# Last mixture of a vision tower: who adds the normalised input, and who adds up the two output sums

## The reference

```python
def _moe(tokens, router_w, w1, b1, w2, b2):
    logits = tokens @ router_w.T
    probs = softmax(logits)
    rw, re = top_k(probs, 2)
    rw = rw / max(rw.sum(-1), 1e-12)
    combine = zeros((N, E)).at[arange(N)[:, None], re].set(rw)
    out = tokens
    for e in range(E):
        hid = gelu(tokens @ w1[e] + b1[e])
        y = hid @ w2[e] + b2[e]
        out = out + combine[:, e:e + 1] * y
    return out
h = h + _moe(_layernorm(h), ...)
```

## Time and profile before

| | |
|---|---|
| median of 3 runs | 734.87 us (733.46 to 735.16) |
| profiled execution | 733.23 us, its span 731.4 us |
| busy over the span | PE 606.9 us (83%), DVE 503.9 (69%), ACT 319.3 (44%), POOL 141.2 (19%) |
| mean granted TensorE clock | 0.928 of full speed |

### The profile page before, as it was taken

How to read it: one execution, slowest core, us unless ns; L and a number is a source line. 1 busy time by engine, 2 the same in 40 slices (tenths; PEclk the granted TensorE clock), 3 DMA queues, 4 the chain that set the end, 5 groups by cost and what they waited for, 6 DMA issues and landing times. The chain is left out here.

```text
span 731.4 us, 17563 instructions
## 1 busy us (share of the span) xinstructions
PE 606.9 (83%) x6943; PEld 377.2 (52%) x6943; DVE 503.9 (69%) x1451; ACT 319.3 (44%) x739; POOL 141.2 (19%) x151
## 2 busy tenths in 40 slices
PE   2999999699975977888887979999955968889884
PEld 2875655489863333444432347787743434444441
DVE  3767789357764547777667327878857688988863
ACT  0100011043322665666665628877941453444441
POOL 1000000465443103221003032431314012220000
PEclk9999999989995799999998899999965799999998
DMA  9998870000000000000000000000000000000001
GB/s 310 411 366 278 293 286 3 1 2 2 2 2 0 1 1 2 2 1 1 3 1 1 1 1 2 2 1 3 1 2 0 5 16 14 17 19 21 20 23 26
DMA packets 28898, 39.19 MB, mean 54 GB/s; under 512 B 19985, under 2 KB 20369, under 8 KB 28817
## 3 DMA queue, kind: packets, MB, share of 16 engines
q1 hardware_dynamic: 19232, 35.46, 13.5%
q10 hardware_dynamic: 9584, 2.61, 1.8%
HBM read 35.37 MB, written 2.69 MB: 52 GB/s over the span
## 5 line engine op out<-in xcount | busy, mean ns | idle before, releaser
L423 POOL TENSOR_TENSOR centred<-h,mean 82x512 f32<-82x512 f32 x64 | 67.4, 1052 | 497.6 <-DVE rstd L412 299.6
L1226 ACT ACTIVATE m_h<-bank,m_b 128x656 f32<-128x656 f32 x112 | 90.4, 807 | 130.2 <-PE bank L1333 130.0
L1556 DVE TENSOR_TENSOR m_hm<-bank,m_h 128x656 f32<-128x656 f32 x112 | 93.7, 836 | 70.5 <-PE bank L1343 70.5
L283 PE MATMUL bank<-cols,tok_weight 64*64 64x328 f32 (+1 forms) x1800 | 114.4, 411 | 16.8 <-DVE cols L321 15.3
L283 PEld LDWEIGHTS bank<-cols,tok_weight 64*64 64x64 f32 x1800 | 76.0, 136 | 52.1 <-issue 17.1
L1333 PE MATMUL bank<-m_xt,m_w 64*64 64x328 f32 x896 | 94.4, 494 | 9.6 <-ACT m_h L1226 8.7
L320 DVE COPY cols<-image 128x1992 f32<-128x1992 f32 x32 | 62.2, 1952 | 16.8 <-DMA image<-in_x_dram 14.7
L1333 PEld LDWEIGHTS bank<-m_xt,m_w 64*64 64x64 f32 x896 | 24.8, 139 | 57.5 <-issue 28.2
L1366 PE MATMUL bank<-m_hm,m_wo 64*64 64x328 f32 x512 | 49.8, 459 | 2.7 <-DVE m_osb L1563 2.3
L813 ACT ACTIVATE sa_prob<-sa_masked,sa_low 82x82 f32<-82x82 f32 x128 | 44.6, 350 | 8.5 <-DVE sa_low L948 8.5
L1343 PE MATMUL bank<-ct,m_sel 64*64 64x328 bf16 x448 | 37.7, 318 | 12.6 <-DVE m_hm L1556 12.2
(11 more groups left out here) (172 smaller groups left out, 1060.9 us busy)
## 6 DMA issues: line engine op xcount, KB each, us to landing
image<-in_x_dram SPq DMA_DIRECT2D x32, 1000.0 KB, 11.1
out_dram<-m_fin SPq DMA_DIRECT2D x16, 164.0 KB
tok_weight<-in_L_tok_weight_dram ACTq DMA_DIRECT2D x2, 400.0 KB, 8.2
m_w<-in_L_ffn_w_dram ACTq DMA_DIRECT2D x2, 128.0 KB
m_sel_raw<-c_sel_dram ACTq DMA_DIRECT2D x1, 256.0 KB
m_w<-in_L_ffn_expert_w_dram ACTq DMA_DIRECT2D x2, 96.0 KB
m_wo<-in_L_ffn_expert_w_dram ACTq DMA_DIRECT2D x4, 48.0 KB
m_sel_raw<-c_sel_dram ACTq DMA_DIRECT2D x1, 192.0 KB
```

Source lines behind the costliest of these rows:

```text
L283: return pe.matmul(sum_bank[u % 2][s][t * D:(t + 1) * D, L * j0:L * j1], weight[s * R:(s + 1) * R, c, :], cols[u % 2][s * R:(s + 1) * R, c ...
L423: pool.tensor_tensor(self.centred[:], slots(self.h, g), mean.broadcast_to([L, G, D]), ALU.subtract).then_inc(self.shifted, 1)
L1226: act.activation(h1[n % RING][:], h1_bank, ACT.Gelu if last else ACT.Relu, bias=W.b1[:, k:k + 1]).then_inc(h1_ready, 1)
L1556: dve.tensor_tensor(hm[k][:], cb_bank, src[n % RING][:], ALU.mult).then_inc(hm_ready, 1)
```

## The change

Pool adds the normalised group to `h` in place (`widen`), right before it normalises the group three further on; the last three follow at the end. VectorE then no longer adds `xt` in `output`: ScalarE copies the even sums from PSUM into a new tile `even` (`output_even`), and VectorE makes `osb` from the odd sums and `even` in one step. `residual` waits for `widened` as well. `copy_x` waits for `h1_done` in both mixtures.

```diff
--- before.py
+++ after.py
@@ -1117,6 +1117,7 @@
         h2 = None if last else [sb(f"h2_{n}", [128, 2, HALF]) for n in range(RING)]
         hm = [sb(f"hm{k}", [128, 2, HALF]) for k in range(NP)]
         osb = sb("osb", [128, HALF])
+        even = sb("even", [128, HALF]) if last else None
         unused = sb("unused", [L, 1])
 
         lg = [sb(f"lg{p}", [L, 2 * G, E]) for p in (0, 1)]
@@ -1154,6 +1155,7 @@
         o_pairs = sem("o_pairs")
         o_done = sem("o_done")
         o_even = sem("o_even")
+        widened = sem("widened")
         o_ready = sem("o_ready")
         o_turned = sem("o_turned")
         added = sem("added")
@@ -1176,11 +1178,21 @@
 
             @block.gpsimd
             def _(pool):
+                def widen(f):
+
+                    pool.wait_ge(normed, f + 1)
+                    pool.tensor_tensor(slots(h, f), slots(h, f), mine.rows(f), ALU.add).then_inc(widened, 1)
+
                 def step(f):
+                    if last:
+                        widen(f - AHEAD)
                     wait(pool, x_turned, f - 2)
                     mine.normalise(pool, f)
 
                 in_groups(step, AHEAD)
+                if last:
+                    for f in range(NG - AHEAD, NG):
+                        widen(f)
                 if following is not None:
                     pool.wait_ge(normed, NG)
                     for f in range(AHEAD):
@@ -1191,10 +1203,7 @@
 
                 def copy_x(f):
                     act.wait_ge(x_turned, f + 1)
-                    if last:
-                        wait(act, o_ready, f - FRONT - 1)
-                    else:
-                        wait(act, h1_done, (f - FRONT - 1) * NP)
+                    wait(act, h1_done, (f - FRONT - 1) * NP)
                     act.activation(xt[f % len(xt)][:], front[:, 0:HALF], ACT.Copy).then_inc(x_ready, 1)
 
                 def router_hidden(f):
@@ -1232,6 +1241,11 @@
                     for s in (0, 1):
                         ins = act.activation(h2[n % RING][:, s, :], h2_bank[:, s, :], ACT.Relu, bias=W.b2[:, s, k:k + 1])
                     ins.then_inc(h2_ready, 1)
+
+                def output_even(g):
+                    act.wait_ge(o_done, g + 1)
+                    wait(act, o_ready, g)
+                    act.activation(even[:], o_banks[0], ACT.Copy).then_inc(o_even, 1)
 
                 def output(g):
                     act.wait_ge(o_done, g + 1)
@@ -1261,6 +1275,8 @@
                             hidden1(g, k + 1)
                         elif exists(g + 1):
                             hidden1(g + 1, 0)
+                        if k == 0 and last and exists(g - 1):
+                            output_even(g - 1)
                         if not last:
                             hidden2(g, k)
                             if k == 0:
@@ -1281,7 +1297,9 @@
                     LayerNorm.after_act(act, g, mine, following)
 
                 in_groups(step)
-                if not last:
+                if last:
+                    output_even(NG - 1)
+                else:
                     output(NG - 1)
 
             @block.tensor
@@ -1558,12 +1576,13 @@
                 def output(g):
                     dve.wait_ge(o_done, g + 1)
                     wait(dve, o_turned, g)
-                    dve.tensor_tensor(osb[:], o_banks[0], xt[g % len(xt)][:], ALU.add).then_inc(o_even, 1)
                     dve.wait_ge(o_even, g + 1)
-                    dve.tensor_tensor(osb[:], o_banks[1], osb[:], ALU.add).then_inc(o_ready, 1)
+                    dve.tensor_tensor(osb[:], o_banks[1], even[:], ALU.add).then_inc(o_ready, 1)
 
                 def residual(g):
                     dve.wait_ge(o_turned, g + 1)
+                    if last:
+                        dve.wait_ge(widened, g + 1)
                     if last and g >= 2:
                         dve.wait_ge(sent[g % 2], g // 2 * 16)
                     dst = fin[g % 2][:] if last else slots(h, g)
```

## The result

The changed kernel takes 757.05 us (754.36 to 760.33, six runs), the kernel before, run beside it, 734.66 us (733.46 to 735.16, six runs): a ratio of 1.031 [1.028, 1.033], 22.4 us slower. The profiled execution took 755.29 us, its span is 753.5 us where it was 731.4. In the later runs 14 of 60 executions of the kernel before took 742 to 752 us, at a lower mean clock; medians are of all executions, and ratios with their intervals of those at most 1.5% above the fastest of their kernel.

The account below looks back on a forecast made before the run. Bound in the last stage by TensorE's spread, VectorE's routing steps stretched by Pool, and the product. Start 3.2, cast bursts 1.64, ranking bursts 1.53, less 0.8 for the sums: +5.6 us, 740.5 us; range 736.5 to 745.5.

Parts of the forecast that it names:

- Direction and place: Last stage: slower by 0.75%, because Pool's adds hold up VectorE's routing steps and TensorE waits for the product.
- One sign: Expected trace sign in the last stage: the period of steps 4 to 8 longer by half a microsecond to 0.8.
- The rival that ends on the other side, the output path wins: Adds shift off the routing steps, only the output sums' gain is left: up to -2.6 us, 732.3 us; chance 0.06.
- the 0.8 us that I summed: Output sums: TensorE's late waits for osb shrink by 0.52, 0.26, 0.03 and about 0.03 us, together -0.8 us.
- Pool's add at 1.04 us: Each of Pool's 16 new 82x512 adds takes 1.04 us, bounds 1.04 and 1.15.
- cast block: Cast bursts: Pool's add stretches VectorE's L1548 from 0.29 to 1.11 us, 0.82 us each, twice.
- ranking block: Ranking bursts: Pool's add delays the end of VectorE's L1522 from 655.18 to 655.69, 0.51 us, three times.
- The start at +3.2 us: Last stage's start: four of six adds each block one more VectorE routing step, 4 x 0.79 us; bounds 1.6 to all four.
- the bursts at 1.64 + 1.53: Adds as third Pool instruction block VectorE's routing: two cast bursts cost 1.64 us, three ranking bursts 1.53; 3.2 in all.
- my 5.6: Whole change: the start's 3.2, cast bursts' 1.64 and ranking bursts' 1.53 less 0.8 for the sums, +5.6 us.
- The clock: TensorE's clock in the last stage: no loss in the forecast sum, though waits for the product grow to 2.0 to 2.1 us.
- two or three more such falls: Rival: TensorE's clock falls two or three more times in the last stage, +3.6 to +5.4 us, 744 to 746; chance 0.15.

Follow-up runs that it names:

- filled pair: The changed kernel and the kernel before, each with six useless TensorE matmuls ahead of the wait for hm in steps 3 to 8: 743.05 and 736.51 us.
- The adds in mid-step: The changed kernel with Pool's adds from group 8 on waiting until a step's output is ready, normalisations unmoved: 749.73 us, ratio 1.017 to the kernel before.
- half-width adds: The changed kernel with each Pool add over half of its group only (82x256): 741.56 us, ratio 1.009 to the kernel before.
- eight tiles with the old normalisations: The changed kernel with eight xn buffers and only the adds moved to mid-step, Pool's normalisations in their old place: 734.65 us, ratio 1.001 to the kernel before.
- filled kernel: The changed kernel with six useless TensorE matmuls ahead of the wait for hm in steps 3 to 8: 743.05 us, ratio 1.012 to the kernel before.

## Why the prediction was wrong in size

*Direction and place.* Right. The adds alone cost as much as the whole change (757.47), everything else gives back 0.8 to 1.5 us (733.65), the blocked steps are L1566 and L1540, and the reduction beside them runs free. One sign failed clearly: the period of steps 4 to 8 was to grow by half a microsecond to 0.8, and went from 10.0 to 10.2 us to 13.3 to 13.5.

*The rival that ends on the other side, the output path wins.* Its mechanism is there, worth the 0.8 us that I summed: osb waits went from 2.3 us to 1.5. Its premise, that the adds shift away from the routing steps, did not come true.

*Pool's add at 1.04 us.* Mis-sized: 1.31 us in the median, 1.26 to 1.39. The adds have two full inputs, the two rows that I took it from read a full and a broadcast one. What follows from the Trainium skill's cycles an element (GPSIMD Engine Reference, 3.1 Elementwise), an estimate of 1.11 us, is short as well; the measurement decides. It made the cast block 0.95 us for 0.82, and the ranking block 0.63 for 0.51.

*The start at +3.2 us and the bursts at 1.64 + 1.53.* The start measured +3.6. The waits for hm grew by 0.13 us in step 3, 0.55 in step 4, 0.95 in each cast step and 0.61 in each ranking step, 3.8 us for my 3.2. With -0.8 this makes 6.6 us for my 5.6, and the filled pair measures 6.5.

*The clock.* This is the step that failed. The sum put the clock at nothing. I wrote that "elsewhere after waits of 1.25 to 1.5 us it stays at 2.4 GHz" and that my waits "grow to 2.0 to 2.1 us", which lies between the two kinds, and then gave "two or three more such falls" at 1.8 us each a chance of 0.15. The waits grew to 2.13 to 2.20 us as forecast. The clock fell in all of steps 2 to 8, five falls more than before, each 6.8 us long and not 3.4, and that cost 15 to 16 us, more than twice the blocks. Two faults in that step: the price of a fall was taken from one fall of the trace before, whose two falls are both 3.4 us long, and waits that recur in every step were treated as separate chances, though here they went together. Had the forecast said "if 2.1 us is enough, it is enough each time", five further falls at 1.8 us would have given 5.6 + 9.0 = 14.6 us; still short, since the falls are longer.

*What stays open.* Why equal waits hold the clock in one execution and not in the next. The adds in mid-step and the kernel before share their waits in steps 4 to 8 within a tenth of a microsecond and not their clock; in the half-width adds 1.59 us was followed by a fall, and 1.61 and 2.69 us were not. That a step at half clock sets up the next one would make the falls keep themselves going, and it fits the adds in mid-step. It does not fit the half-width adds, where falls in steps 4, 5 and 6 were followed by none, nor the profile of eight tiles with the old normalisations (743.03 us), where the fall behind the 1.50 us wait of step 4 stayed the last. No run here isolates what decides.

## What to carry to other kernels

In these traces a Pool tensor_tensor holds up VectorE's operations with two SBUF inputs until it ends (1.24 us for 0.29), and its f32 to bf16 casts too (1.15 for 0.36). It leaves the reductions (0.28) and the operations with a PSUM operand (0.83, 0.67, 0.21) alone. So where a Pool instruction stands matters more than how many there are. Taking work off an engine that is not late there buys next to nothing (16 VectorE sums of 0.49 us gave 0.8 us back). And a longer wait of TensorE has to be priced twice, by its length and by the clock behind it. When it recurs in each step, work out the loss for a fall in every step as well as for none, since these runs show both and cases between, and test it by filling the wait with matmuls.

## What the hardware showed that I had not expected

- Pool's 82x512 tensor_tensor takes 1.31 us (1.26 to 1.39) with two full inputs, where the two with one broadcast input take 1.04; over 82x256 it takes 0.77. In the changed kernel's trace the five adds of 1.37 to 1.39 are those that start while a cast of VectorE still has 0.25 us to run.
- Useless matmuls in six waits made the changed kernel 14.0 us faster (743.05 for 757.05), with no other edit.
- The half-clock stretches in the changed kernel are 6.8 to 6.9 us long, twice those of the kernel before, though the waits ahead of the last five are shorter (2.1 to 2.2 us) than the 3.11 us ahead of the fall before. Ahead of step 2's fall the wait is 2.96 us in both kernels, and the stretch 3.4 us in one and 6.8 in the other.
- One execution of the filled kernel ran at a mean clock of 0.552 and took 1032.84 us; in ten further ones it did not come again.
